# Attention with another order of matmuls, seven tiles of exponentials and three units of queries

## What is computed

```python
x = x + _L0_xattn_ref(_layernorm(x), ctx_1024, ctx_1024, mask, gamma, beta)
y = _layernorm(x)
q = (y @ qw + qb).reshape(B, S, 16, 32).transpose(0, 2, 1, 3)
k, v = y @ kw + kb, y @ vw + vb          # 4 heads each, used by 4 query heads
scores = jnp.einsum('bhqd,bhkd->bhqk', q, k) / np.sqrt(32)
attn = jax.nn.softmax(scores, axis=-1)
out = jnp.einsum('bhqk,bhkd->bhqd', attn, v)
src = rmsnorm(y + out.reshape(B, S, 512) @ ow + ob) ; src = src + moe(src) ; x = x + rmsnorm(src)
```

## Time and profile before

| | us |
|---|---|
| median of 3 runs | 3328.96 |
| lowest, highest | 3324.41, 3328.96 |
| profiled execution | 3330.29 |
| its span, first to last instruction | 3328.6 |
| projection, to the first matmul of attention | 336.94 |
| first B of attention | 373.08 |
| first B of the last unit | 2198.06 |

### The profile page before, as it was taken

The page is one execution under the profiler, slowest core; times in us unless marked ns, Lnnn a source line. Parts: engine busy times, 40 slices in busy tenths (PEclk is TensorE's granted clock), DMA queues, the critical chain, the costliest instruction groups (busy, mean ns, idle before and its releaser), DMA issues. The chain is left out here.

```text
span 3328.6 us, 45557 instructions
## 1 busy us (share of the span) xinstructions
PE 3118.0 (94%) x16824; PEld 2009.6 (60%) x16824; DVE 2122.1 (64%) x3807; ACT 1614.3 (48%) x3249; POOL 2026.7 (61%) x878
## 2 busy tenths in 40 slices
PE   6898899999999999999999999984999999999992
PEld 4675444544544544544545445532999999889992
DVE  6786788788788788788788787833233333333334
ACT  3332366566566566556566565662343333334332
POOL 3432599899899899899899899893011111111114
PEclk8998799999999999999999999996999999999996
DMA  3544632010101113011011011003333333333237
GB/s 124 201 166 148 173 114 111 23 33 24 45 23 45 37 36 74 20 33 43 17 36 44 13 37 41 14 20 113 84 93 71 77 90 69 99 73 92 51 77 265
DMA packets 135520, 245.50 MB, mean 74 GB/s; under 512 B 30263, under 2 KB 35383, under 8 KB 132773
## 3 DMA queue, kind: packets, MB, share of 16 engines
q1 hardware_dynamic: 117232, 206.56, 19.3%
q0 software_dynamic: 16640, 35.42, 6.0%
q10 hardware_dynamic: 1461, 1.11, 0.1%
HBM read 127.82 MB, written 117.57 MB: 74 GB/s over the span
## 5 line engine op out<-in xcount | busy, mean ns | idle before, releaser
L1159 ACT ACTIVATE p_PR<-p_ps_b 128x512 f32<-128x512 f32 x2048 | 1066.4, 602 | 709.9 <-PE p_ps_b L1453 691.0
L1240 DVE TENSOR_REDUCE home_mxp<-p_ps_a 128x1 f32<-128x512 f32 x2012 | 1261.0, 681 | 212.7 <-PE p_ps_a L1439 201.6
L1021 POOL TENSOR_TENSOR p_PP<-p_PP,p_PR 128x2048 f32<-128x2048 f32 x223 | 1022.9, 4587 | 37.8 <-ACT p_PR L1159 14.4
L1439 PE MATMUL p_ps_a<-home_K,home_Q 96*128 96x512 f32 x2012 | 809.8, 431 | 23.6 <-DVEq L1254 11.5
L1453 PE MATMUL p_ps_b<-home_Q,home_K 98*128 98x512 f32 x2048 | 755.4, 416 | 11.8 <-DMA home_Q<-p_ml 6.0
L1439 PEld LDWEIGHTS p_ps_a<-home_K,home_Q 96*128 96x128 f32 x2012 | 376.7, 191 | 448.9 <-DVE home_mxp L1240 313.1
L1017 POOL TENSOR_TENSOR p_PP<-p_PR 128x2048 f32<-128x2048 f32 x127 | 582.5, 4587 | 101.1 <-ACT p_PR L1159 86.8
L1717 POOL DMA_INDIRECT src_d<-p_YE,p_token x80 | 124.2, 1553 | 832.8 <-DVE p_YE L1843 632.7
L1453 PEld LDWEIGHTS p_ps_b<-home_Q,home_K 98*128 98x128 f32 x2048 | 387.4, 190 | 207.3 <-ACT p_PR L1159 117.2
L1463 PE MATMUL p_ps_pv<-p_PR,p_VS 128*32 128x512 f32 x4096 | 511.7, 600 | 0.0
L1762 ACT ACTIVATE p_hf<-p_ps_h 128x384 f32<-128x384 f32 (+1 forms) x256 | 112.3, 439 | 577.2 <-PE p_ps_h L85 571.2
(11 more groups left out here) (194 smaller groups left out, 3267.4 us busy)
## 6 DMA issues: line engine op xcount, KB each, us to landing
weights_w_raw<-in_L_ffn_w SPq DMA_DIRECT2D x16, 2048.0 KB, 8.9
xe_d<-p_SR SPq DMA_DIRECT2D x20, 1056.0 KB, 9.7
home_Q<-qh_d SPq DMA_DIRECT2D x64, 256.0 KB, 3.8
p_XE<-xe_d SPq DMA_DIRECT2D x16, 792.0 KB, 4.7
src_d<-p_SR SPq DMA_DIRECT2D x9, 1024.0 KB, 6.3
p_XE<-xe_d SPq DMA_DIRECT2D x16, 528.0 KB, 3.7
p_X<-in_x SPq DMA_DIRECT2D x8, 1024.0 KB, 8.0
x_d<-p_x SPq DMA_DIRECT2D x8, 1024.0 KB, 5.4
```

Source lines behind the costliest of these rows:

```text
L1021: nc.gpsimd.tensor_tensor(PP[:, buf, :, :], PP[:, buf, :, :], PR[:, tile_at(u, tile), :, :], ALU.add).then_inc(add_made, 1)
L1159: nc.scalar.activation(PR[:, tile_at(u, kt), j, :], ps_b[:, n % BK, :], ACT.Exp, scale=SCALE).then_inc(ex_made, 1)
L1240: nc.vector.reduce_max(mxp[:, a // (S // CH), a % (S // CH):a % (S // CH) + 1], ps_a[:, bank, :], AXX).then_inc(a_read, 1)
L1439: nc.tensor.matmul(ps_a[:, bank, :], QS[g][0:96, j, t * P:(t + 1) * P], KS[g][0:96, kb * CH:(kb + 1) * CH], start=True, stop=True).then_in ...
```

## The change

- **Orders.** `BASE` has other strings with the same letters; `EXTRA` is as before. V's and D's stand together more often, M stands between two B's in place of behind three V's, and the A's are 2 to 7 for each kt in place of 3 to 5.
- **Lateness and room.** `V_LATE` is 4, `PK` is 7. The queries have `QK` = 3 buffers, used by unit in turn; SP loads unit u + 3 when the scores of u are done and no longer waits for its values, other than for keys and values of the second batch.
- **The seam.** `LED` is 27: three lead blocks at each place. SP sends the first maxima behind the loads of g = 1 and before those of g = 2; g = 3 is loaded after unit 0. The low part of the output weight is taken inside unit 0, one quarter at each of kt 1 to 4, PE waits for it only after chunk 0, and POOL clears `SR[:, 0]`. The output weight waits in the last tile of `PR`, and ACT waits for it at kt 6 of unit 0.
- **Projection.** Two of the four tiles of `attention` stand before the first projection, on PE and on ACT.
- `PR` comes first in SBUF, and a tile `end` of its width keeps the place behind it.

```diff
-            first, n = {"1": (0, 3), "4": (3, 3), "values": (6, 6)}.get(part) or (12 + 4 * int(part[4:]), 4)
-            return range(first, first + n)
+            first = {"1": 0, "4": 3, "values": 6}[part] if part in ("1", "4", "values") else 9 + 3 * int(part[4:])
+            return range(first, first + 3)
...
     transposes(c - 1, y, y_made, y_tr, yl_made, (2, 3))
+                attention(c, (0, 1), c == 0)
...
                     project(c - 1, 0, c == 1)
-                attention(c, c == 0)
+                attention(c, (2, 3), c == 0)
...
-    BASE = ["VABBABAB", "AVABAABBAB", "AVABABBAB", "VABBBAABA", "DABBABAAB", "ABBAVVBAB", "BAABBABV", "VAABABBAB",
-            "VABAABBAB", "VVAABABBAB", "VAABBABABAV", "DABABBAAB", "ADABBAABB", "ABADABABAB", "ABBABABAVVVM", "BABBAABAD"]
+    BASE = ["ABABBAB", "ABVVBABABA", "BAABBABAV", "VDABBABAABAVAA",
+            "BBAABBA", "BVABABAB", "BABABAB", "VVABABBAB",
+            "VBABBAB", "AABABVVABABAA", "BBABAVB", "AADABABBABA",
+            "BBAABVDVABA", "ADABABABAB", "ABBABMBAVVA", "ABABABBAD"]
-    TURN, V_LATE, D_LATE = 13, 3, 1
+    TURN, V_LATE, D_LATE = 13, 4, 1
...
-    AK, BK, PK = 3, 3, 6
+    AK, BK, PK = 3, 3, 7
+    QK = 3
...
-    LED = 36
+    LED = 27
...
-                    if not last:
+                    if unit(c, g) + QK < NU:
                         hold(sc_mm, NSC * (unit(c, g) + 1))
-                        hold(pv_mm, KT * (unit(c, g) + 1))
-                        load(nxt, g)
+                        load(*divmod(unit(c, g) + QK, KV))
...
-            for g in range(1, KV):
-                load(0, g)
+            load(0, 1)
...
-            maxima_to(0, 1)
+            maxima_to(0)
+            load(0, 2)
...
+                        if first and g == 0 and 0 < kt <= KV:
+                            split_out_weight(kt - 1)
```

More of the change, by code:

```diff
@@ L346, in probabilities_out, with attention_out @@
                 nc.scalar.activation(prT[:], ps_pt[0:CT, :], ACT.Copy).then_inc(prT_made, 1)
-            def attention_out(c, first=False):
+            def attention_out(c, ts, first=False):
                 if not first:
                     act.wait_ge(x1_made, TT * c)
-                for t in range(TT):
+                for t in ts:
                     act.wait_ge(o_mm, TT * c + t + 1)
@@ L620, in probabilities, with attention @@
                 last.then_inc(p_tr, 1)
-            def attention(c, first=False):
+            def attention(c, ts, first=False):
                 pe.wait_ge(prT_made, c + 1)
-                for t in range(TT):
+                for t in ts:
                     if not first or t >= 2:
@@ L745, in phase_attend @@
     NS = len(GROUPS)
-    assert D_LATE == 1 and GROUPS[-1] == tuple(range(KT - V_LATE, KT))
+    assert D_LATE == 1 and min(GROUPS[-1]) >= KT - V_LATE
     ADDS = sorted((tiles[k], n, k) for n, tiles in enumerate(GROUPS) for k in range(1, len(tiles)))
@@ L899, in load @@
                 for part, src in ((0, qh_d), (1, qh_d), (2, ql_d)):
[L900 removed]
+                    sp.dma_start(f32(QS[unit(c, g) % QK][32 * part:32 * part + 32, :, :]),
                                  src[bass.ds(c, 1), heads, :].rearrange("a (j d) q -> d (a j) q", d=HD)).then_inc(q_in[g], 16)
[L902 to L907 removed]
+                if c % CB == 0:
+                    if c > 0:
+                        hold(sc_mm, NSC * (unit(c, g) - KV + 1))
+                        hold(pv_mm, KT * (unit(c, g) - KV + 1))
+                    for part, src in ((0, kh_d), (1, kl_d), (2, kh_d)):
+                        sp.dma_start(f32(KS[g][32 * part:32 * part + 32, :]).rearrange("d (n q) -> d n q", n=CB),
+                                     src[bass.ds(row, CB), HD * g:HD * (g + 1), :].rearrange("n d q -> d n q")).then_inc(q_in[g], 16)
+                    load_values(row, g)
             def load_y(c):
@@ L1143, in _ @@
                 nc.scalar.activation(ow_hi[:, g, :], ow_raw[:, g, :], ACT.Copy).then_inc(owh_made, 1)
-            act.wait_ge(owl_made, KV)
             def exp(c, g, kt, j, first):
                 u = unit(c, g)
+                if j == 0 and first and kt == PK - 1:
+                    act.wait_ge(owl_made, KV)
                 if j == 0:
@@ L1452, in scores @@
                     pe.wait_ge(ex_made, n - BK + 1)
[L1453 removed]
+                nc.tensor.matmul(ps_b[:, n % BK, :], KS[g][:, kt * P:(kt + 1) * P], QS[unit(c, g) % QK][:, j, :],
                                  start=True, stop=True).then_inc(sc_mm, 1)
@@ L1595, in _ @@
             pe.wait_ge(fold_made, DK - 1)
+            body(0, first=True)
             pe.wait_ge(owl_made, KV)
-            body(0, first=True)
             for c in range(1, NC - 1):
@@ L1947, in others @@
     def others(self, s):
-        self.QS = [self.Q0] + [s.sb(f"Q{g}", [98, G, CH], F32R) for g in range(1, KV)]
+        self.QS = [self.Q0] + [s.sb(f"Q{i}", [98, G, CH], F32R) for i in range(1, 3)]
         self.KS = [self.K0] + [s.sb(f"K{g}", [98, S], F32R) for g in range(1, KV)]
@@ L2066, in build_layer @@
         with Scope(nc, "kept") as s:
+            s.sb("end", [P, G, CH])
             norm_row, norm_in = s.sb("norm_row", [P, D]), s.sem("norm_in")
```

50 lines of the change are left out of this document (22 added, 28 removed).

## The result

| | before | after |
|---|---|---|
| median (4 runs each on the same chip) | 3327.67 | 3299.44 |
| lowest to highest | 3324.41 to 3328.96 | 3297.72 to 3303.64 |
| span of the profiled execution | 3328.6 | 3301.9 |
| projection, to the first A of attention | 336.94 | 309.07 |
| first A to first B | 36.14 | 32.33 |

The ratio is 0.9919 (95% interval 0.9901 to 0.9936). The forecast was 3268 with a range of 3242 to 3298. The sign is right and the size is not: of 60.9 us the trace shows 26.7. The table says where. All of the gain, 31.7, came ahead of the first B, where 29.3 had been forecast, and attention, from which 31.6 had been forecast, gave nothing: from its first B to its last V it took 3.9 us more.

A forecast was written before the change was run, and what follows sets the result against it. PE was taken as the bound, 53.3 of letters and 1.7 of stalls in a unit, with POOL as late in g = 3. Terms 27.6 + 4.0 + 4.3 + 13 + 12 = 60.9 off 3329.0 gave 3268.1, range 3242 to 3298.

The forecast's parts named there:

- perhaps 0.5, lies under this: Unit g = 2: the router's bank is needed two letters sooner; its wait costs perhaps 0.5, under POOL's bound.
- I put 3: Unit 0: output-weight subtractions on DVE meeting POOL's adds, at most two of four, cost 3 (bounds 0 and 8).
- I keep 0.4: Units of attention: of the other 0.8 of stalls, where B waits for ACT or A for its bank, 0.4 remains.
- The stall around M: Each unit: with M between B's and two V's behind it, the stall behind M goes, about 0.9.
- dense A's: Rival, chance 0.04: at kt 3, 9 and 11 DVE frees banks late, PE stands 4.5 a unit; 3389.
- Without POOL the closing D of g = 3 would come 2.3 earlier: Units g = 2 and 3: POOL's chain lets this D gain only 0.56; both units together gain 1.4, not 3.2.
- less one V (0.9): Last chunk: its end is POOL's and one V more follows it, 0.9 off; the last chunk gains 2.8.
- The lead blocks: Early stage: three in a row in place of four avoid waits for banks; gain 13 (bounds 8 and 16).
- the cross attention: Projection: two attention tiles fill PE's wait of 1.54 in 7 chunks; 9, with clock 12 (bounds 4 and 19).
- the seam: Ahead of the first B: the maxima's low part is sent sooner; gain 4.3 (bounds 0 and 6).
- I take half: Projection: four slow chunks lose 1.5 each to a lowered clock; half of that 6 comes back, 3.
- Attention keeps its pace: Rival, chance 0.14: the stall behind M only moves; attention gives 6 in place of 31.6; 3293.

The follow-up runs named there:

- e2: Changed kernel with one V moved ahead of the A's behind the router's N in g = 2, tile 2: 3281.7 us, 0.9872.
- e3: Changed kernel with output weight's low part on POOL ahead of its adds, and V ahead of the A's behind N in g = 2: 3275.6 us, 0.9840.
- e4: Changed kernel with the four output-weight subtractions on DVE, all ahead of unit 0: 3288.7 us, 0.9887.
- e1: Changed kernel with the output weight's low part taken by POOL ahead of its adds, not by DVE: 3290.3 us, 0.9894.
- e5: Changed kernel with the old strings and V_LATE = 3: 3306.7 us, 0.9936.
- e13: Changed kernel with old strings, V_LATE = 3, M between B's, e1's edit, and the last unit's D of tiles 9 to 12 behind the last V: 3278.3 us, 0.9845.
- e14: e3 with DVE's maxima over half of each bank, half of their input left out: 3246.6 us, 0.9758.
- e10: e3 with POOL adding only two of four heads, half of the sums left out: 3261.5 us, 0.9797.
- e7: Changed kernel with the cross attention's four tiles together behind the first projection again: 3314.3 us, 0.9965.

## Why the prediction failed

Counting from the first B to the last V, 31.6 were forecast and 3.9 lost. The missing 35.5 are: 22.0 in chunks 1 to 6, 5.4 in unit 0, 3.4 in units 1 to 3, and 4.8 in the last chunk.

**The router's wait, "perhaps 0.5, lies under this": the step that failed most.** It was taken as a wait of 0.45 that grows a little and hides under POOL's bound. It became 1.17 and brought stretches at half clock; 2.6 in a full chunk on the mean, 0.9 where the clock stayed at 1.00, 17.7 in all (e2). None of it lay under POOL's bound: in the chunk shown the closing D of g = 3 comes 114.8 after the first B of g = 2, and 111.4 in e3, later by what g = 2 is longer. Of the 22.0 it makes 15.5. The prediction had the pieces: rows 7 show what a wait of 1.54 does to the clock of the projection. It used that for the projection and not here.

**Unit 0, "I put 3": the meeting cost 10.0.** Mechanism and place were right. But not two but three subtractions met an add, PE stood 5.8 in all, and the clock was lowered to between 0.5 and 0.7 up to 370, which the sum had no term for. e4 and e1 take the term apart: the subtractions without a meeting cost 1.7 (1.5 forecast), the meeting 10.0, over its bound of 8. The rest of the change gave unit 0 2.7 where the sum had 0.9; it had left out the order's gain for this unit without a reason. Together unit 0 grew by 9.0 (3.6 forecast).

**"I keep 0.4" of the other stalls: wrong.** By the prices of the prediction a clean unit before is 53.3 of letters and 1.7 of stalls. The stall around M went, as forecast (e5 to e13: 54.96 to 54.1 by M alone, 0.85; e13's other edits touch other units). But the other 0.8 stayed whole (e13: 54.1 against 53.3), and the new strings have 1.5 of it (54.5 against 53.0). The difference is mostly A's of the denser places that come 0.09 to 0.14 late, seven in a unit of e3 and one in e13. They go when DVE's reductions are shortened (e14), so they are DVE's banks. No wait of PE shows it; it is in the weight load, which waits for DVE and then does not hide behind the matmul ahead. In the changed kernel the load and the matmul of such an A, which elsewhere start 0.23 apart, start together:

```profile
526.68 0.19 PEld L1452 LDWEIGHTS p_ps_a<-home_K,home_Q 96*128 96x128 f32 x1 [0.28 <-DVE home_mxp L1253]
526.68 0.50 PE L1452 MATMUL p_ps_a<-home_K,home_Q 96*128 96x512 f32 x1
```

That is the rival "dense A's": its condition is met, in small change, at 0.7 in a unit and not 4.5. Its own sum was off too: the 14 letters of kt 3 take 5.8 and not 4.9, so DVE has more room there than it says; but five of the A's stand within 2.0 us, closer than 0.60 each. So units 1 to 3 gained 0.5 and not 1.6. That the tiles with A's in close order pay at each A and not only once DVE is late by a bank is what the sum lacked. At the steps at B's the trace names ACT's exponential as what the weight load waits for, in six of seven in the changed kernel:

```profile
538.45 0.19 PEld L1466 LDWEIGHTS p_ps_b<-home_Q,home_K 98*128 98x128 f32 x1 [0.26 <-ACT p_PR L1172]
```

No run shortened the exponentials, so that these steps are ACT's is read from the trace and not tried.

**POOL's limit: its size.** "Without POOL the closing D of g = 3 would come 2.3 earlier": without POOL it came 0.2 earlier (e10). With POOL it was to gain 0.56, and the V behind it 0.88. Counted from the first B of g = 2 this D stood at 111.0 before on the mean, at 111.2 in e3 and 111.1 in e13: it gained nothing, and what g = 2 and 3 together gained in e3, 0.7 and not 1.4, lies behind it, where a V is gone. Nor did PE's wait for POOL at this D grow by 1.5 to 2; it is 0.4 at most in the changed kernel. PE's own letters hold both units at 112.05, 0.35 below e3: the limits of POOL and PE lie close together, and the sum knew only one. In e13, where PE is faster, POOL takes 1.5 to 3.4 in g = 3.

**The tail, "less one V (0.9)": 3.2.** POOL works through the last unit without a pause, and starts on it 0.65 ahead of the unit's first B, where it started 1.48 ahead before. So its closing add comes 0.9 later in the unit's time (54.9 against 54.1), and the one V more behind it is the 0.9 forecast. The other 1.4 are the clock: PE idles 5.57, and this D and the V's behind it begin at half clock, where the clock was at 1.00 before. The prediction named POOL as the end there and counted only the V.

**Ahead of the first B: right, and low.** The lead blocks were worth 14.0 (13), the cross attention 16.5 (12, everything 19), the seam 3.8 (4.3). In the trace 31.3 came from chunk 2 on and 3.5 were lost ahead of it by where this execution's start fell. The lowered clock of the projection left with the wait wholly; the step that failed here is "I take half".

The Trainium skill ("TensorE: Matmul & The Clock Gate", HAM oscillation — how this bites in real kernels) says that recurring idle lowers the clock and filling it keeps the clock up. The trace agrees in the projection, where by e7 the whole 6 us came and not half, and in g = 2, where the clock fell behind a wait of 1.17 in six units of seven and stayed at 1.00 in all when the wait was filled (e2). The page's own case has longer waits, for DMAs; here 1.54 and 1.17 were enough. There and in unit 0 the same rule speaks against the change, which the prediction did not ask.

**The rivals.** "Attention keeps its pace" (3293) had the nearest time for the wrong reason: a clean unit gained 0.5, g = 0 and 1 gained 1.15 and 1.55 (why they gained more than a clean unit was not tried), and two places lost it again. With both repaired the time is 3275.6, and with the last D moved 3270.

## What to carry to other kernels

A wait of PE is to be priced with the clock behind it: 1.17 us cost 0.9 where the clock held and up to 3.9 where it fell, and 1.54 cost 1.8 or 3.5. When an order is changed, list each wait that the old order just covered (the router's 0.45) and ask of each what covers it now, before adding up gains elsewhere. And letters closer together than DVE's 0.60 for each bank pay about 0.1 each by an unhidden weight load, before a wait appears under PE.
